# Four-layer graph network on one core: one-hot blocks handed to ScalarE in the third edge stage, and 32 more made columns, picked by VectorE's one-hot blocks, in the last

## The reference

```
L2 (attention):   q = feats@Wq+bq;  k = feats@Wk+bk;  v = feats@Wv+bv
                  score = exp(clip(sum(k[src]*q[dst]) / 8, -5, 5))
                  wv = segment_sum(v[src]*score, dst) / (segment_sum(score, dst) + 1)
                  h = feats@Wf + bf + wv@Wo + bo;  return h + layer_norm(h)
L3 (relations):   s[r, n] = segment_sum(node_feats[src] * norm, (etype, dst))
                  h = relu(sum_r s[r] @ W[r] + bias) + relu(node_feats@res_w.T + res_b)
                  return batch_norm(h)         # 64 relations, W[r] is 64x64
```

## Time and profile before

| | us |
|---|---|
| runs: lowest, median, highest | 4991.7, 4992.75, 4993.47 |
| the profiled execution's own time | 4994.97 |
| its span | 4992.8 |
| third edge stage, first to last gather's start | 3035.2 to 3828.1 |
| last edge stage, first MSG to the end of the last scan | 4076.8 to 4916.5 |
| busy over the span: TensorE, VectorE, ScalarE, GpSimd | 3904.1, 4035.4, 2091.6, 3669.7 |

### The profile page before, as it was taken

The page is one execution under the profiler, slowest core; times in us unless marked ns, Lnnn a source line. Parts: engine busy times, 40 slices in busy tenths (PEclk is TensorE's granted clock), DMA queues, the critical chain, the costliest instruction groups (busy, mean ns, idle before and its releaser), DMA issues. The chain is left out here.

```text
span 4992.8 us, 56860 instructions
## 1 busy us (share of the span) xinstructions
PE 3904.1 (78%) x17000; PEld 2737.1 (55%) x17049; DVE 4035.4 (81%) x5762; ACT 2091.6 (42%) x3734; POOL 3669.7 (73%) x3384
## 2 busy tenths in 40 slices
PE   2788888872999999999999946888883656677651
PEld 1455555542888888888888834333441433333321
DVE  4788889874899999999999956999997647677663
ACT  0577777751344444444444423555554322222221
POOL 6777777764788888888888727777776567777774
PEclk6899999995999999999999957999996778888875
DMA  8788888853788888888888734444443662222221
GB/s 305 248 285 285 286 282 283 283 209 136 285 322 317 324 318 324 316 325 315 325 316 326 277 73 125 136 135 137 135 127 102 265 228 70 66 68 73 66 62 44
DMA packets 359635, 1074.18 MB, mean 215 GB/s; under 512 B 100998, under 2 KB 124354, under 8 KB 315012
## 3 DMA queue, kind: packets, MB, share of 16 engines
q1 hardware_dynamic: 241524, 852.49, 45.8%
q0 software_dynamic: 102208, 156.10, 12.2%
q10 hardware_dynamic: 15696, 63.31, 3.1%
HBM read 678.05 MB, written 392.57 MB: 214 GB/s over the span
## 5 line engine op out<-in xcount | busy, mean ns | idle before, releaser
L1880 PE MATMUL COLS<-CF,XF 128*128 128x256 f32 x6272 | 1485.9, 380 | 6.0 <-DVE XF L1988 6.0
L1880 PEld LDWEIGHTS COLS<-CF,XF 128*128 128x128 f32 x6272 | 1135.1, 190 | 130.2 <-DVE XF L1988 6.4
L1137 ACT ACTIVATE OUT<-SC 128x576 f32<-128x576 f32 (+3 forms) x392 | 577.0, 1472 | 1114.0 <-DVE SC L1072 754.7
L1847 POOL DMA_INDIRECT G<-x_tab,SRC x784 | 835.5, 1066 | 228.9 <-issue 212.6
L1020 POOL DMA_INDIRECT G<-xl_tab,SRC x752 | 721.5, 959 | 229.2 <-issue 224.1
L1020 POOL DMA_INDIRECT G<-rel_tab,REL x672 | 643.1, 957 | 205.0 <-issue 205.0
L1020 POOL DMA_INDIRECT G<-kv_tab,SRC x608 | 601.0, 989 | 193.2 <-issue 172.8
L1457 PE MATMUL PICK<-HOT,X 125*128 125x512 bf16 x2200 | 530.1, 405 | 143.9 <-ACT TURNED L1495 127.2
L1629 PE MATMUL MADE<-XM,W 128*128 128x512 f32 x896 | 486.6, 701 | 162.3 <-DVE XM L1717 162.2
L1457 PEld LDWEIGHTS PICK<-HOT,X 125*128 125x128 bf16 x2200 | 225.1, 103 | 434.3 <-issue 205.3
L1629 PEld LDWEIGHTS MADE<-XM,W 128*128 128x128 f32 x896 | 196.3, 228 | 431.7 <-issue 231.6
(11 more groups left out here) (313 smaller groups left out, 7163.5 us busy)
## 6 DMA issues: line engine op xcount, KB each, us to landing
SHB<-ea9t SPq DMA_DIRECT2D x196, 1024.0 KB, 9.7
wkv_tab<-WKV SPq DMA_DIRECT2D x98, 1024.0 KB, 6.2
WKV<-wkv_tab SPq DMA_DIRECT2D x98, 1024.0 KB, 6.0
scan<-OUT SPq DMA_DIRECT2D x196, 288.0 KB
scan<-OUT ACTq DMA_DIRECT2D x98, 576.0 KB
rel_tab<-YS SPq DMA_DIRECT2D x50, 1024.0 KB
RAW<-spread SPq DMA_DIRECT2D x196, 256.0 KB, 2.8
spread_q<-ZQ SPq DMA_DIRECT2D x98, 512.0 KB
```

What stands on the lines that cost most here:

```text
L1137: nc.scalar.activation(self.OUT[d][:, :, 0:WD], SC[b][:, 0:WD, 1:1 + C].rearrange("p r j -> p j r"), ACT.Copy).then_inc(self.copied_out, 1)
L1847: pool.indirect_dma_start(out=e.G[0][b][:, col, :], out_offset=None, in_=x1_tab, in_offset=bass.IndirectOffsetOnAxis(ap=SRC[:, at:at + 1], ...
L1880: nc.tensor.matmul(acc, XF[b][:, k, edges_], CF[:, k, :], start=(k == 0), stop=False)
```

## The change

**Third edge stage.** Four of the 25 one-hot blocks of each batch (21 to 24) are made by ScalarE: Abs of index minus node number, then Relu of one minus that, in three pieces in three of four chunks, between `place` and OUT. VectorE's quarters shrink to 6, 5, 5 and 5. TensorE begins a batch with ScalarE's blocks. `take` moves one chunk earlier, `narrow` too.

**Last edge stage.** The made columns become 144, in 18 batches over the same 88 chunks. Fourteen batches still gather their x rows one stage earlier (112 gathers, as before). Batches 5, 9, 13 and 17 get theirs by one-hot blocks: VectorE compares 512 source indices at a time with 25 node numbers (`compare`, 5 blocks before a mask, 40 such groups, spread from mask 14 to mask 255 of 288), TensorE picks behind that mask's multiply into one bank (`pick`, 10 matmuls), ScalarE copies each half out (`take_half`), and `turn` folds the pieces. X3 is built again in this stage: GpSimd clears a part and numbers the nodes, ScalarE copies the high and the middle piece, VectorE makes REST and the low piece. SyncE loads the source indices of a half (`load_half`). The type buffers TYPE8, UPPER and CODE become single, and the next batch's types are read behind `take` instead of those of the batch after it. The edge weights EW move into the PSUM tile of MSG, to free a bank. The rest of the diff is semaphores and shapes.

```diff
...
-BATCHES3 = 14
+BATCHES3 = 18
+PICKED3 = [5, 9, 13, 17]
...
+GATHERED3 = [i for i in range(BATCHES3) if i not in PICKED3]
+GATHERED_COLS = [MADE_COLS[8 * i + q] for i in GATHERED3 for q in range(8)]
+HALVES3 = [(i, h) for i in PICKED3 for h in range(2)]
+PICK_BEFORE = {16 * (i - 5) + 14 + 5 * g + 4 * (g >= 5): 10 * n + g for n, i in enumerate(PICKED3) for g in range(10)}
...
-                        for j, (t, c) in enumerate(MADE_COLS):
+                        for j, (t, c) in enumerate(GATHERED_COLS):
...
-                QUARTERS = [range(0, 7), range(7, 13), range(13, 19), range(19, 25)]
+                QUARTERS = [range(0, 6), range(6, 11), range(11, 16), range(16, 21)]
+                BY_ACT = [(21, 22), (23,), (24,)]
...
+                        def pick_by_act(i):
+                            wait(pe, act_compared, 3 * i + 3)
+                            wait(pe, taken, i)
+                            for k in range(21, K):
+                                ins = pick_rows(k, k == 21, False)
+                            ins.then_inc(act_read, 1)
...
+                            pick_by_act(i)
...
+                        def compare_by_act(i, part):
+                            ks = BY_ACT[part]
+                            if part == 0:
+                                wait(act, narrowed, i + 1)
+                                wait(act, act_read, i)
+                            wait(act, act_compared, 3 * i + part)
+                            for a, k in enumerate(ks):
+                                nc.scalar.activation(AWAY[N, a, :], ID16[i % 2][N, :], ACT.Abs,
+                                                     bias=MINUS_NODE[N, k - 21:k - 20]).then_inc(away, 1)
+                            wait(act, away, 4 * i + (2, 3, 4)[part])
+                            nc.scalar.activation(HOT[N, ks[0]:ks[-1] + 1, :], AWAY[N, 0:len(ks), :], ACT.Relu,
+                                                 bias=ONES[N, 0:1], scale=-1.0).then_inc(act_compared, 1)
...
-                            if t % PERIOD == 0 and 1 <= t // PERIOD <= BATCHES:
-                                take(t // PERIOD - 1)
+                            if t % PERIOD == 3 and t // PERIOD < BATCHES:
+                                take(t // PERIOD)
+                            elif t % PERIOD != 3 and t // PERIOD + 1 < BATCHES:
+                                compare_by_act(t // PERIOD + 1, t % PERIOD)
                             e.store_rows(act, t, n, b, t < 4)
-                            if t % PERIOD == 3 and t // PERIOD + 2 < BATCHES:
+                            if t % PERIOD == 2 and t // PERIOD + 2 < BATCHES:
                                 narrow(t // PERIOD + 2)
...
-                                for k in (ks[0:4], ks[4:])[part]:
+                                for k in (ks[0:3], ks[3:])[part]:
...
-                TYPE8 = e.pair("TYPE8", [P, 8 * P], I32)
-                UPPER, CODE = e.pair("UPPER", [P, 8 * P]), e.pair("CODE", [P, 8 * P])
+                TYPE8 = sb("TYPE8", [P, 8 * P], I32, ctx)
+                UPPER, CODE = sb("UPPER", [P, 8 * P], F32, ctx), sb("CODE", [P, 8 * P], F32, ctx)
...
+                        def load_half(h):
+                            wait(sp, narrowed, h)
+                            sp.dma_start(SRC_HALF[:, :], src_half[h:h + 1, :].to_broadcast([P, 512]))\
+                              .then_inc(src_half_in, 16)
...
+                        nc.gpsimd.iota(NODE[:, :], [[1, K]], base=0, channel_multiplier=K).then_inc(blank, 1)
+                        nc.gpsimd.memset(X3[:, :, 1, 64:128], 0.0).then_inc(blank, 1)
...
                         def turn(i):
-                            wait(pe, doubled, i + 1)
                             wait(pe, masked, MASKS * i)
+                            if i in PICKED3:
+                                wait(pe, half_taken, 2 * PICKED3.index(i) + 2)
+                                for h in range(2):
+                                    ins = nc.tensor.matmul(XT8[:, 512 * h:512 * h + 512],
+                                                           FOLD[:, :, :].rearrange("p a f -> p (a f)"),
+                                                           PICKED[:, 512 * h:512 * h + 512], start=True, stop=True)
+                                ins.then_inc(x_turned, 1)
...
+                        def pick(g):
+                            h, part = divmod(g, 5)
+                            wait(pe, compared, g + 1)
+                            if part == 0:
+                                wait(pe, half_taken, h)
+                            for k in range(5 * part, 5 * part + 5):
+                                for piece in range(2):
+                                    ins = nc.tensor.matmul(PICK[:, :], X3[N, k, piece, :], HOT[g % 2][N, k % 5, :],
+                                                           start=(k == 0 and piece == 0),
+                                                           stop=(k == K - 1 and piece == 1))
+                            ins.then_inc(picked, 1)
...
                                 multiply(i, c)
+                                if MASKS * i + c in PICK_BEFORE:
+                                    if MASKS * i + c == min(PICK_BEFORE):
+                                        wait(pe, blank, 2)
+                                        wait(pe, x_low, 1)
+                                    pick(PICK_BEFORE[MASKS * i + c])
...
+                        def take_half(h):
+                            i, half = HALVES3[h]
+                            wait(act, picked, 5 * h + 5)
+                            if h == 0:
+                                wait(act, x_low, 1)
+                            if h >= 2 and half == 0:
+                                wait(act, x_turned, PICKED3[h // 2 - 1] + 1)
+                            nc.scalar.activation(PICKED[:, 512 * half:512 * half + 512], PICK[:, :], ACT.Copy)\
+                              .then_inc(half_taken, 1)
...
+                        def compare(g):
+                            h, part = divmod(g, 5)
+                            if g == 0:
+                                wait(v, x_low, 1)
+                            wait(v, narrowed, h + 1)
+                            wait(v, picked, g - 1)
+                            for k in range(5 * part, 5 * part + 5):
+                                ins = nc.vector.tensor_scalar(HOT[g % 2][N, k % 5, :], ID16[N, :], NODE_F[N, k:k + 1],
+                                                              None, ALU.is_equal)
+                            ins.then_inc(compared, 1)
...
+                                wait(v, x_high, 1)
+                                nc.vector.tensor_tensor(REST, X[:, :, :], X3[:, :, 0, 0:64], ALU.subtract).then_inc(x_rest, 1)
+                            if t == 2:
+                                wait(v, x_middle, 1)
+                                nc.vector.tensor_tensor(X3[:, :, 1, 0:64], REST, X3[:, :, 0, 64:128], ALU.subtract)\
+                                  .then_inc(x_low, 1)
...
                                     take(i)
-                                    if i + 2 < BATCHES3:
-                                        read_types(i + 2)
+                                    if i + 1 < BATCHES3:
+                                        read_types(i + 1)
                             for j in range(MASKS_AT[t], MASKS_AT[t + 1]):
+                                if j in PICK_BEFORE:
+                                    compare(PICK_BEFORE[j])
                                 mask(j)
...
```

More of the change, by code:

```diff
@@ L1448, in _, with pick_rows @@
                     def _(pe):
+                        def pick_rows(k, first, last):
+                            for piece in range(2):
+                                for half in range(2):
+                                    edges_ = slice(512 * half, 512 * half + 512)
+                                    ins = nc.tensor.matmul(PICK[:, edges_], X3[N, k, piece, :], HOT[N, k, edges_],
+                                                           start=(first and piece == 0), stop=(last and piece == 1))
+                            return ins
+                        def pick_by_act(i):
[4 more added lines that the diff above has]
+                            ins.then_inc(act_read, 1)
                         def pick(i, q):
                             wait(pe, compared, 4 * i + q + 1)
-                            if q == 0:
-                                wait(pe, taken, i)
                             for k in QUARTERS[q]:
[L1454 to L1459, removed]
+                                ins = pick_rows(k, False, k == 20)
                             ins.then_inc(read, 1)
@@ L1506, in _ @@
                         narrow(1)
+                        wait(act, negated, 1)
+                        for part in range(3):
+                            compare_by_act(0, part)
                         wait(act, e.ready, e.N_READY)
@@ L1572, in edges_3 @@
```

(10 more changed lines are left out.)

103 lines of the change are left out of this document (74 added, 29 removed).

## The result

The changed kernel takes 5060.8 us (median of four runs, 5059.22 to 5063.97), the kernel before 4992.67 us beside it: a ratio of 1.0138, 95% interval 1.0123 to 1.0152. It is 68 us slower; 51 had been forecast. The profiled execution has a span of 5059.2 us.

The account below looks back on a forecast made before the run. GpSimd bound both stages before; in the last, VectorE chained with TensorE would become the bound. +60 (last stage) - 9 (third) = +51 us on the profiled 4994.97, 5046; that run being 2.2 us above the median, 5044; range 4990 to 5095.

Parts of the forecast that it names:

- its own list: Signs to look for, mainly in the last stage: GpSimd's gaps ending with SC, changed VectorE waits, batches at 46 to 49 us.
- -9 forecast: Third edge stage: 8 us of waits and 3 us of shorter gathers gained, 2 us charged for ScalarE; bounds -12 and +44.
- The 8 us of GpSimd's waits: Third edge stage: GpSimd's true waiting for VectorE's scan, 8 us, would be gained.
- ScalarE's lateness: Third edge stage: ScalarE's added blocks cost 2 us; at most 44 us, if 2 us late in each of 22 batches.
- The 3 us: Third edge stage: 88 fewer comparisons shorten gathers by 3 us, a share of 19 us excess for 550 comparisons.
- The lower bound of -12: Third edge stage: the lower bound of the forecast of -9 us.
- +60 forecast: Last edge stage: VectorE chained with TensorE needs 47.4 us a batch, GpSimd 39.2; the stage ends at 4977 against 4916.5.
- 7.2 + 1.2: Last edge stage, per batch: VectorE's stall before TURNED, 9.8 less 2.6 us of sums, plus 1.2 us on average for picks.
- TensorE keeps the full clock: Rival, last stage: picks fill TensorE's idle time, the wait is 8.1 us, not 9.8; 29 us less, 5015; chance 0.12.
- ScalarE binds the third stage: Rival, third edge stage: ScalarE's lateness costs the full +44 us, 5090; chance 0.04.
- GpSimd remains the bound: Rival, last stage: VectorE gets through 4.89 chunks in 39.2 us, so the kernel is faster, 4946; chance 0.06.
- TensorE falls behind: Rival, last stage: at half clock the picks push TensorE 3 us behind per batch, +48 us, 5092; chance 0.07.

Follow-up runs that it names:

- run 3: The changed kernel, but TensorE turns the next batch behind multiply 15 instead of ahead of multiply 12: 4982.99 us, 0.9978 of before.
- run 4: The kernel before, with TensorE's turn of the next batch moved behind multiply 15 from ahead of multiply 12: 4996.97 us, 1.0007 of before.
- run 10: The kernel before with the third stage's whole part, but from the third batch on ScalarE's Abs and Relu 8 columns wide, not 1024: 4972.31 us, 0.9955 of before.
- run 8: The kernel before with the third stage's comparisons split the new way and 80 of 550 left out, their blocks made by nobody: 4980.33 us, 0.9975 of before.
- run 9: The kernel before with 80 of the third stage's 550 comparisons left out and the old split kept: 4986.31 us, 0.9981 of before.
- run 1: The kernel before with the third stage's part of the change alone, the last stage as before: 4971.87 us, 0.9957 of before.
- run 6: The changed kernel, but TensorE multiplies one of a group's five blocks, 320 of 400 pick matmuls left out: 5059.38 us, 1.0137 of before.

## Why the prediction was right, and where it was not

The direction and the mechanism hold. The rule that it was built on, that the last stage would turn from GpSimd's into that of VectorE chained with TensorE, is what the traces show, and runs 3 and 4 show it from both sides. By its own list: the gaps of GpSimd in the last stage end with SC (135.0 us of 321.3, the rest the ordinary issue), MSG's wait fell below 60 us (39.8), TURNED's rose above 110 (134.7), the batches follow at 48.0 us where 46 to 49 stood, the comparisons count 462.

The size was 17 us short: 30 us too little in the last stage and 13 too little gain in the third. That they partly cancel is luck.

**The third stage, -9 forecast, -22 measured.** The 8 us of GpSimd's waits went as said, and ScalarE's lateness, charged with 2 us and bounded by 44, cost nothing (run 10). The comparisons alone return 7 to 13 us, waits included (runs 8 and 9), and my 8 + 3 = 11 lies within that. What the sum has no term for is the order: the copy and the narrowing one chunk earlier, which I took for free, with ScalarE's blocks first on TensorE, seem to be worth some 10 us (run 10 against runs 8 and 9). The 3 us is not confirmed as a size either. In the profile after the gathers are 601.0 - 586.3 = 14.7 us shorter, and the excess that it was a share of was taken too small: against the median of 0.944 us it is 27 us, not 19, since the 0.957 us of the last stage holds gathers lengthened beside the reading of the types. The lower bound of -12 stood on the same share, and was too narrow. The lock for the whole instruction, which the Trainium skill states (SBUF — State Buffer, section "SBUF: two separate sides"), would by an estimate have returned up to 39 us for the comparisons alone; the 7 to 13 us of runs 8 and 9 lie far below that.

**The last stage, +60 forecast, +90 measured.** The first TURNED comes 54.2 us after the first MSG (54.9 forecast). From the first to the last it takes 816.1 us against 793.8: 22 us more, 1.3 a batch. The comparisons were well priced at 0.30 us (five take 1.54 us in the timeline), the masks and sums are those of before. The wait before TURNED with its picks was put at 7.2 + 1.2, 8.3 us on the mean over the batches; it is (134.7 - 8.5) / 17 = 7.4, the first one left out. What I had no term for is a second and a third place where VectorE waits inside a batch: for a free XM tile (15.9 / 17 = 0.9 us), the longest of them behind the turn back, and for placed columns (11.6 / 17 = 0.7 us), because ScalarE stood 19 to 23 us before `take_half` and places them only after it, four times. The prediction had put ScalarE's half copies into the time that it waits for the scan; the copies of 0.6 us fit, but the wait for the pick that stands before them in program order does not. No run moved `take_half`. With the (10.3 - 6.8) / 17 = 0.2 us for rows that makes 46.7 - 0.9 + 0.9 + 0.7 + 0.2 = 47.6 of 48.0. The prediction's stall was worked out as if TensorE were late once a batch. When VectorE no longer waits for rows, it catches TensorE and ScalarE at each place where they are behind. The turn of a picked batch, 3.78 us against 1.09 or 1.97 for transposes, had no term either; it is inside the 7.4.

The tail behind the last TURNED is 59.3 us, not 51.7. I let GpSimd be four chunks ahead there, with 34 gathers to go 5 us later. The trace has 44 gathers after it, from 4924.75 to 4978.42 + 0.94, 54.6 us, and from there 4.1 us to the end of the scan.

**The rivals.** *TensorE keeps the full clock* was right in its mechanism, at a chance of 0.12, and wrong in its time. Eleven of 13 turns run at the high rate, and the undisturbed wait is 5.6 us, where the 8.1 less 2.6 us of that rival give 5.5. But the same picks that keep the clock up lie in the wait of the other batches. My 7.2 us were nearly right as a mean over several kinds of batches that I had not seen, which is luck. The Trainium skill (TensorE: Matmul & The Clock Gate, "What's actually happening") has the clock low by default and raised by activity; the turns of run 6, slow again once the picks are gone, agree. *ScalarE binds the third stage* is refuted by runs 1 and 10, *GpSimd remains the bound* by the 135.0 us. *TensorE falls behind* is there in part, as the 15.9 us before XM.

What would have caught the miss is the neighbour of the term that I worked out: the order of TensorE's work. The prediction named the stall, even its cause, a turn that holds four multiplies. It did not ask what the new batches would be worth without it: 43.6 us, still above GpSimd's 39.2 with 18 batches; with 16 or 17, where GpSimd needs 45.4 or 42.2 us, the two meet.

## What to carry to other kernels

When work moves from the engine that binds to one with spare time, look for the instruction that waits in program order with ready work behind it: as long as another engine binds it is invisible, and the moment the bound moves it sets the pace. Work out the batch of the new chain first, and shift only as much as balances the two engines; here 16 or 17 batches with the turn moved give 29 to 32 us, 22 of them from the third stage, where 18 without the move lost 68. A stall that is a mean over batches of several kinds should be looked at batch by batch before it is used as one number.

## What the runs showed of the hardware that was not expected

Taking 320 of 400 picks away from TensorE gained nothing (5059.38 against 5060.8 us), since the granted clock fell with them: over the same window from 4108 to 4846 us it is 0.91 with the picks and 0.85 without, and the multiplies' busy time over the whole stage goes from 561.8 to 581.2 us:

```profile
4108.00:4846.00 738.00, 602.47 (x1698) 277.64 (x1698) 586.00 (x707) 153.11 (x290) 471.12 (x492) 0.91 0.24 63
```

```profile
4108.00:4846.00 738.00, 567.39 (x1392) 267.20 (x1393) 585.63 (x708) 153.68 (x292) 468.56 (x491) 0.85 0.24 64
```

VectorE's comparisons lengthen GpSimd's gathers by amounts that are not fixed by their number. A gather takes 0.944 to 0.946 us in the median of every kernel. In the third stage of before the 608 together take 27 us more than that (601.0 - 608 x 0.944), and all of it lies beside comparisons: each of the 181 gathers that are over 0.02 us longer than the median overlaps one in time, and the 319 gathers that overlap none take 0.944 us on the mean. In the profiles of runs 8 and 9, with 80 comparisons fewer, the excess is 22 and 15 us. In the last stage the reading of the types does the same: beside line 1708 of the kernel before a gather took up to 1.73 us.
